# Non-local attention block: theta and phi projected with packed weight halves, and a unit matmul for the correction

## The reference

```python
theta = einsum('bhwc,cd->bhwd', x, W_theta)          # 1024 pixels x 32
phi = maxpool2x2(einsum('bhwc,cd->bhwd', x, W_phi))  # 256 keys x 32
g = maxpool2x2(einsum('bhwc,cd->bhwd', x, W_g))      # 256 keys x 128
beta = softmax(einsum('bqd,bkd->bqk', theta, phi))
tmp = einsum('bqk,bkv->bqv', beta, g)
return gamma * einsum('bhwv,vc->bhwc', tmp, W_o) + x
```

## Time and profile before

| what | value |
|---|---|
| median of 3 runs | 248.03 us (247.55 to 249.0) |
| the profiled execution | 248.0 us, of which the span of the trace is 246.2 us |
| instructions | 4332 |
| busy: PE, DVE, POOL, ACT | 96%, 84%, 69%, 60% of the span |
| clock granted to TensorE | 1.0 |

### The profile page before, as it was taken

How to read it: one execution, slowest core, us unless ns; L and a number is a source line. 1 busy time by engine, 2 the same in 40 slices (tenths; PEclk the granted TensorE clock), 3 DMA queues, 4 the chain that set the end, 5 groups by cost and what they waited for, 6 DMA issues and landing times.

```text
span 246.2 us, 4332 instructions
## 1 busy us (share of the span) xinstructions
PE 235.7 (96%) x1464; PEld 210.4 (85%) x1464; DVE 205.8 (84%) x473; ACT 148.1 (60%) x275; POOL 168.7 (69%) x119
## 2 busy tenths in 40 slices
PE   7896999999999999999999999999999999999884
PEld 4675888898989889898989989898998989899774
DVE  4587896988989898898989899898989989898855
ACT  3763865847475684847567484747749474735260
POOL 1596588676868677686958767695876779544480
PEclk9999999999999999999999999999999999999999
DMA  6790009549194775919377592928668391906924
GB/s 221 285 393 18 3 1 313 204 104 386 49 311 177 234 284 124 384 63 337 123 209 303 142 365 77 347 101 270 243 218 296 95 357 70 329 14 226 372 88 173
DMA packets 15078, 51.14 MB, mean 208 GB/s; under 512 B 1872, under 2 KB 2512, under 8 KB 15056
## 3 DMA queue, kind: packets, MB, share of 16 engines
q1 hardware_dynamic: 14368, 50.14, 58.2%
q10 hardware_dynamic: 688, 0.72, 0.8%
HBM read 33.95 MB, written 16.78 MB: 206 GB/s over the span
## 4 chain that ended last, share of the span: by engine, by line
PE 80%; DVE 7%; DMA 4%; ACT 3%; POOL 3%; issue 1%; ACTq 0%; DVEq 0%
PE proj L195 30%; PE out L299 24%; PE shift L299 8%; PE shift L272 6%; PE score L229 5%; PE score L256 4%; DVE neg_parts L577 3%; DMA x_t<-in_xt 2%; POOL e_lo L506 2%; DMA theta<-neg_lo 2%; PE shift L195 1%; DVE out L552 1%; DVE theta L558 1%; POOL x_lo L501 1%; PE proj L188 1%
## 5 line engine op out<-in xcount | busy, mean ns | idle before, releaser
L506 POOL TENSOR_TENSOR e_lo<-e_sb,e_hi 128x512 fp32r<-128x512 f32 x64 | 82.0, 1295 | 50.8 <-ACT e_sb L434 50.8
L501 POOL TENSOR_TENSOR x_lo<-x_t,x_hi 128x1024 fp32r<-128x1024 f32 x31 | 74.3, 2398 | 13.7 <-ACT x_hi L391 13.7
L299 PE MATMUL out<-G_hi,e_lo 128*128 128x258 f32 x188 | 53.2, 283 | 0.5 <-POOL e_lo L506 0.5
L299 PE MATMUL out<-G_hi,e_hi 128*128 128x258 f32 x188 | 53.4, 284 | 0.0
L299 PE MATMUL out<-G_lo,e_hi 128*128 128x258 f32 x188 | 53.3, 283 | 0.0
L603 DVE SCALAR_TENSOR_TENSOR y_sb<-out,r_sum,x_n 128x256 f32<-128x256 f32 x94 | 45.5, 484 | 6.4
L195 PE MATMUL proj<-x_hi,w_hi 128*128 128x512 f32 x122 | 48.4, 396 | 2.3 <-DVE theta L558 2.3
L195 PE MATMUL proj<-x_hi,w_lo 128*128 128x512 f32 x122 | 48.3, 396 | 0.0
L195 PE MATMUL proj<-x_lo,w_hi 128*128 128x512 f32 x122 | 48.2, 395 | 0.0
L431 ACT ACTIVATE e_hi<-shift 128x512 fp32r<-128x512 f32 x64 | 38.5, 601 | 13.5 <-PE shift L272 13.5
L577 DVE TENSOR_REDUCE neg_parts<-score 128x2 f32<-128x512 f32 x64 | 43.6, 685 | 1.3 <-PE score L229 0.4
(11 more groups left out here) (81 smaller groups left out, 386.3 us busy)
## 6 DMA issues: line engine op xcount, KB each, us to landing
x_n<-in_xn SPq DMA_DIRECT2D x32, 512.0 KB, 7.3
x_t<-in_xt SPq DMA_DIRECT2D x31, 512.0 KB, 5.3
out<-y_sb SPq DMA_DIRECT2D x31, 512.0 KB, 6.6
x_t<-in_xt ACTq DMA_DIRECT2D x2, 256.0 KB, 4.7
w_sb<-in_w_proj SPq DMA_DIRECT2D x1, 256.0 KB, 3.7
theta<-neg_hi ACTq DMA_DIRECT2D x16, 4.0 KB
theta<-neg_lo SPq DMA_DIRECT2D x16, 4.0 KB
out<-y_sb SPq DMA_DIRECT2D x1, 256.0 KB, 2.4
```

Source lines behind the costliest of these rows:

```text
L299: last = nc.tensor.matmul(out_bank(i, t)[:, 0:GW], e[:, i % 2, KC * h + k, cells], G[:, i % 3, k, :], start=(n == 0), stop=(n == 3 * KC - 1))
L501: nc.gpsimd.tensor_tensor(x_lo[:, i % 2, h], x_t[:, i % 2, h], x_hi[:, i % 2, h].bitcast(f32), ALU.subtract).then_inc(x_lo_ready, 1)
L506: nc.gpsimd.tensor_tensor(e_lo[:, i % 2, n, :], e_sb[:, n, :], e_hi[:, i % 2, n, :].bitcast(f32), ALU.subtract).then_inc(e_lo_ready, 1)
```

## The change

The theta/phi weight of the host becomes W_theta, W_phi side by side (64 columns), and the split weights go into one tile `w_all`: 64 high columns, then their 64 remainders, then g's high and low parts. `pair(i, h)` replaces `theta_phi`: for each chunk one matmul of x_hi with all 128 columns gives the high product in PSUM rows 0 to 63 and the correction (x_hi times the weight's remainder) in rows 64 to 127; for each chunk one matmul of x_lo with the 64 high columns adds to rows 0 to 63. ACT copies rows 64 to 127 to SBUF (`copy_corr`), and `add_corr` adds them to rows 0 to 63 by a matmul with a 64x64 unit matrix. A half thus takes five matmuls where it took six. ACT casts 32 rows of theta, not 96, and theta's second high copy (rows 64 to 95) is made by a transfer within SBUF, issued by SP (`twin`), for which `scores(i, 0)` waits.

The order changes too. In the loop PE has `scores(b, h)` ahead of the projection and `add_corr(a, h)` behind `shifted(d, 2 + h)`; ACT has both copies, theta casts and `phi_high` woven with the exponentials of d; DVE has `maxima(b, 0)` first and `maxima(b, 1)` after the second `theta_low`. In the head the first loads all come from SP (x, then weights, then x), DVE splits the weights in parts and makes x_lo of the whole first image, W_o is split later, and `theta_low(1, 1)` stands ahead of `neg_low(0)`. The core of the diff:

```diff
-PROJ = P + DV
+PAIR = 2 * DK
+PROJ = PAIR + DV
+VHI, VLO = 2 * PAIR, 2 * PAIR + DV
+PACKED = VLO + DV
...
+            def twin(i):
+                sp.wait_ge(theta_hi_ready, 2 * i + 2)
+                sp.dma_start(theta[2 * DK:THETA, i % 3, :].bitcast(f32),
+                             theta[0:DK, i % 3, :].bitcast(f32)).then_inc(theta_twin[i % 3], 16)
...
+            for h in range(2):
+                load_t(2, h)
             for h in range(2):
                 load_n(0, h)
+            twin(0)
             for h in range(2):
                 load_t(3, h)
+            twin(1)
             max_into_stack(0)
             for s in range(2, B):
                 a, b, d = s, s - 1, s - 2
+                twin(a)
...
+            def pair(i, h):
+                if i == 0 and h == 0:
+                    pe.wait_ge(w_pair_lo_ready, 1)
+                elif i == 1:
                     pe.wait_ge(theta_lo_ready, h + 1)
                     pe.wait_ge(phi_pooled, h + 1)
                 elif i > 1:
                     pe.wait_ge(g_pooled, 2 * (i - 1) + h + 1)
-                pe.wait_ge(x_lo_ready, 2 * i + h + 1)
-                project(i, h, 0, proj[h], tp_ready)
+                if i > 0 or h > 0:
+                    pe.wait_ge(x_lo_ready, 2 * i + h + 1)
+                for c in range(CC):
+                    if i == 0 and h == 0:
+                        pe.wait_ge(x0_hi_ready, c + 1)
+                    last = nc.tensor.matmul(proj[h][:, :], w_all[:, c, 0:P], x_hi[:, i % 2, h, c, :],
+                                            start=(c == 0), stop=(c == CC - 1), skip_group_check=True)
+                last.then_inc(corr_ready, 1)
+                for c in range(CC):
+                    if i == 0 and h == 0:
+                        pe.wait_ge(x0_lo_ready, c + 1)
+                    nc.tensor.matmul(proj[h][0:PAIR, :], w_all[:, c, 0:PAIR], x_lo[:, i % 2, h, c, :],
+                                     start=False, stop=False, skip_group_check=True)
+
+            def add_corr(i, h):
+                if i == 0 and h == 0:
+                    pe.wait_ge(eye_ready, 1)
+                pe.wait_ge(corr_copied, 2 * i + h + 1)
+                nc.tensor.matmul(proj[h][0:PAIR, :], eye[:, :], corr[:, h, :],
+                                 start=False, stop=True, skip_group_check=True).then_inc(tp_ready, 1)
...
+                    pe.wait_ge(theta_twin[i % 3], twins(i))
...
                 a, b, d = s, s - 1, s - 2
                 if s > 2:
                     for h in range(2):
-                        theta_phi(a, h)
                         scores(b, h)
+                        pair(a, h)
                         shifted(d, 2 + h)
+                        add_corr(a, h)
                     for h in range(2):
                         values(a, h)
                         scores(b, 2 + h)
...
             def theta_high(i, h):
                 act.wait_ge(tp_ready, 2 * i + h + 1)
-                nc.scalar.copy(theta[0:THETA, i % 3, HALF * h:HALF * (h + 1)],
-                               proj[h][0:THETA, :]).then_inc(theta_hi_ready, 1)
+                nc.scalar.copy(theta[0:DK, i % 3, HALF * h:HALF * (h + 1)],
+                               proj[h][0:DK, :]).then_inc(theta_hi_ready, 1)
+
+            def copy_corr(i, h):
+                act.wait_ge(corr_ready, 2 * i + h + 1)
+                nc.scalar.copy(corr[:, h, :], proj[h][PAIR:P, :]).then_inc(corr_copied, 1)
...
+            nc.scalar.copy(eye[:, :], ident[0:PAIR, 0:PAIR]).then_inc(eye_ready, 1)
+            copy_corr(0, 0)
             x_high(0, 1)
-            act.wait_ge(wog_ready, 1)
-            nc.scalar.copy(wo_hi[:, :], w_og[:, :]).then_inc(wo_hi_ready, 1)
+            x_high(1, 0)
             theta_high(0, 0)
-            x_high(1, 0)
+            copy_corr(0, 1)
             x_high(1, 1)
             theta_high(0, 1)
             phi_high(0)
+            copy_corr(1, 0)
+            act.wait_ge(wog_ready, 1)
+            nc.scalar.copy(wo_hi[:, :], w_og[:, :]).then_inc(wo_hi_ready, 1)
             theta_high(1, 0)
+            copy_corr(1, 1)
             g_high(0)
             x_high(2, 0)
             theta_high(1, 1)
             x_high(2, 1)
+            neg_high(0)
             phi_high(1)
-            neg_high(0)
             G_high(0)
             g_high(1)
...
+            copy_corr(2, 0)
             exps(0, 0)
             exps(0, 1)
+            theta_high(2, 0)
+            copy_corr(2, 1)
+            G_high(1)
             theta_high(2, 1)
-            G_high(1)
+            exps(0, 2)
             phi_high(2)
-            exps(0, 2)
             exps(0, 3)
             for s in range(2, B):
                 a, b, d = s, s - 1, s - 2
                 if s > 2:
-                    for h in range(2):
-                        theta_high(a, h)
-                        exps(d, 2 + h)
+                    copy_corr(a, 0)
+                    theta_high(a, 0)
+                    copy_corr(a, 1)
+                    exps(d, 2)
+                    theta_high(a, 1)
                     phi_high(a)
+                    exps(d, 3)
...
             def theta_low(i, h):
-                rows, pixels = slice(DK, 2 * DK), slice(HALF * h, HALF * (h + 1))
+                pixels = slice(HALF * h, HALF * (h + 1))
                 dve.wait_ge(theta_hi_ready, 2 * i + h + 1)
-                v.tensor_tensor(theta[rows, i % 3, pixels], proj[h][rows, :], theta[rows, i % 3, pixels].bitcast(f32),
+                v.tensor_tensor(theta[DK:2 * DK, i % 3, pixels], proj[h][0:DK, :], theta[0:DK, i % 3, pixels].bitcast(f32),
                                 ALU.subtract).then_inc(theta_lo_ready, 1)
...
+            thin, wide = slice(0, PAIR), slice(PAIR, PROJ)
+            dve.wait_ge(w_in, 16)
+            split_hi(thin, thin, w_pair_hi_ready)
+            split_lo(slice(PAIR, 2 * PAIR), thin, thin, w_pair_hi_ready, w_pair_lo_ready)
+            split_hi(slice(VHI, VHI + DV), wide, w_g_hi_ready)
+            first_x_low(0)
+            split_lo(slice(VLO, VLO + DV), wide, slice(VHI, VHI + DV), w_g_hi_ready, w_g_lo_ready)
+            first_x_low(1)
+            dve.wait_ge(x_hi_ready, 1)
+            v.tensor_tensor(x_lo[:, 0, 1], x_t[:, 0, 1], x_hi[:, 0, 1].bitcast(f32),
+                            ALU.subtract).then_inc(x0_lo_ready, 1)
...
             phi_pool(1, 1)
+            theta_low(1, 1)
             neg_low(0)
-            theta_low(1, 1)
             phi_low(1)
...
                 a, b, d = s, s - 1, s - 2
                 if s > 2:
+                    maxima(b, 0)
                     for h in range(2):
                         phi_pool(a, h)
                         theta_low(a, h)
-                        maxima(b, h)
+                    maxima(b, 1)
                     phi_low(a)
                     for h in range(2):
```

More of the change, by code:

```diff
@@ L211, in values @@
                     pe.wait_ge(phi_pooled, 2 * i + h + 1)
-                project(i, h, P, value_bank(i, h), g_ready)
+                elif h == 0:
+                    pe.wait_ge(w_g_lo_ready, 1)
+                for c in range(CC):
+                    for n, (w, x) in enumerate(((VHI, x_hi), (VLO, x_hi), (VHI, x_lo))):
+                        last = nc.tensor.matmul(value_bank(i, h)[:, :], w_all[:, c, w:w + DV], x[:, i % 2, h, c, :],
+                                                start=(c == 0 and n == 0), stop=(c == CC - 1 and n == 2))
+                last.then_inc(g_ready, 1)
             def scores(i, n):
                 if n == 0:
+                    pe.wait_ge(theta_twin[i % 3], twins(i))
                     pe.wait_ge(theta_lo_ready, 2 * i + 2)
@@ L310, in _ @@
                 nc.tensor.matmul(score[0][:, :], e_lo[:, 1, 3, 0:P], e_lo[:, 1, 3, :], start=True, stop=True)
-            first_project()
+            pair(0, 0)
             values(0, 0)
-            theta_phi(0, 1)
+            add_corr(0, 0)
+            pair(0, 1)
             values(0, 1)
-            theta_phi(1, 0)
+            add_corr(0, 1)
+            pair(1, 0)
             scores(0, 0)
             scores(0, 1)
-            theta_phi(1, 1)
+            add_corr(1, 0)
+            pair(1, 1)
             scores(0, 2)
             scores(0, 3)
+            add_corr(1, 1)
             values(1, 0)
@@ L326, in _ @@
             values(1, 1)
-            theta_phi(2, 0)
+            pair(2, 0)
             shifted(0, 0)
@@ L331, in _ @@
             shifted(0, 1)
-            theta_phi(2, 1)
+            add_corr(2, 0)
+            pair(2, 1)
             mix(1)
@@ L335, in _ @@
             shifted(0, 2)
+            add_corr(2, 1)
             values(2, 0)
@@ L609, in _, with split_hi, split_lo, first_x_low @@
             v.memset(G_lo[:, :, :, C:GW].bitcast(f32), 0.0).then_inc(fixed_ready, 1)
-            dve.wait_ge(w_in, 16)
-            v.tensor_copy(w_hi[:, :, :], w_sb[:, :, :]).then_inc(w_hi_ready, 1)
-            dve.wait_ge(w_hi_ready, 1)
```

(10 more changed lines are left out.)

35 lines of the change are left out of this document (20 added, 15 removed).

## The result

The changed kernel takes 266.74 us (median of 4 runs, 266.12 to 269.03) against 248.51 (4 runs, 247.55 to 249.62): ratio 1.074, interval 1.067 to 1.081. It is 18.2 us slower. The prediction had the sign, and was 14 us too low and outside its range. The profiled execution took 269.03 us, with a span of 267.0 and a mean granted clock of 0.97, so it is 2.3 us above the median. In it one 4 KB transfer in the tail takes 4.04 us, against 2.60 us in the earlier trace rows.

A forecast was written before the change was run, and what follows sets the result against it. The prediction took PE to bound the loop; 248.0 us, plus 5.0 for longer loop stages, plus 0.1 for the last stage, minus 0.5 in the head, gave 252.6 us, range 243.0 to 261.0.

The forecast's parts named there:

- the sign: Whole kernel: slower, chance 0.65, against 0.10 for the same time and 0.25 for faster.
- PE bounds the loop: Loop stages: PE sets the pace, busy for 99.60 of 99.60 us over seven stages.
- every matmul fewer is worth its spacing if nothing else becomes late: Theta/phi projections: 0.232 us saved per half, 7.4 us for 16 images, if PE stays the bound.
- The round trip of the copy: Each projection half: PE to ACT's 0.58 us copy to add_corr on PE, a wait of 0.13 each.
- the spacing behind the unit matmul: Loop stage: the next matmul follows add_corr at the usual 0.23, scores(b,1) at 1.76 after add_corr at 1.53.
- +0.13: ACT in the loop: exponentials of (d,2) start 0.13 later per stage if nothing overlaps the copy; outside the main sum.
- The wait of values(a, 1): Loop stage: PE waits 0.30 for DVE's theta remainder, behind ACT's late second theta cast.
- Rival 3: PE projections: changing matmul shape on the array costs 0.16, four times a half; some 260.7 us, chance 0.18.
- the landing of the twin: Head: image 0's theta transfer lands near 16.4, losing 0.9; head in sum -0.5, from -2.2 to +1.5.
- The gain of 1.4 in the head: Head, DVE: theta_low(1,1) ahead of neg_low(0) starts 1.4 us sooner, so values(1,1) wait less for it.
- Costed at nothing: ACT's 32 more casts, the 32-row theta cast, the loop's twin transfers, early scores, DVE's order; the tail also 0.
- Rivals 1 and 2: 1: corrections hidden, PE stays the bound, 240.1 or 244.3, chance 0.25. 2: waits cancel the saving, 247 to 249, chance 0.10.

The follow-up runs named there:

- e7: Kernel before with one of the six matmuls of each theta/phi half left out (x_hi chunk 1 with the weight's remainder): 245.69 us, ratio 0.989.
- e6: e5 without ACT's copy of the correction; the unit matmul adds zeros and waits for nothing: 247.77 us, ratio 0.995.
- e5: Changed kernel with the unit matmul padded to 128 rows and image 0's second theta copy made by ACT casts, not a transfer: 258.60 us, ratio 1.038.
- e3: Changed kernel with image 0's second theta copy made by two ACT casts instead of the transfer: 260.70 us, ratio 1.046.
- e2: Changed kernel with the first unit matmul of an image moved behind scores(b,1) in the loop, still 64 rows: 266.80 us, ratio 1.072.
- e11: Kernel before with 31 added matmuls of 64 rows, one ahead of each theta/phi half but the first, result overwritten: 264.01 us, ratio 1.060.
- e12: Kernel before with 31 added matmuls of 128 rows and 64 weight columns, placed as in e11, result overwritten: 253.14 us, ratio 1.018.
- e8: Kernel before with two head swaps: theta_low(1,1) ahead of neg_low(0) on DVE, neg_high(0) ahead of phi_high(1) on ACT: 247.96 us, ratio 0.998.

## Why the prediction was wrong

The account of the 18 us, from the medians: the saved matmuls give 3.6 (e7 against before); the rest of the new program without the copy costs 2.1 (e6 against e7, and e6 starts its first `turn_max` 2.1 later); the copy 10.8 (e5 against e6); the 64 rows 2.1 once the head is mended (e3 against e5) or 3.4 alone; image 0's transfer 6.0. In sum +17.4, against 18.2 measured; the runs come from different chips, and before is 0.8 slower on that of e7. The intervals of the ratios leave each term uncertain by some 2 us.

- **PE bounds the loop** was right, and "every matmul fewer is worth its spacing if nothing else becomes late" was the right condition. Half the saving was out of reach even with nothing added (e7): theta's remainder gained only 0.23, the slack of 0.11 was used up, and the wait brought a late weight load.
- **The round trip of the copy** was sized well. The copy took 0.58 as taken, the first unit matmul started 1.54 into the stage (predicted 1.53), with a wait of 0.14 (0.13).
- **The step that failed in the loop** is the spacing behind the unit matmul: scores(b, 1) at 1.76 were to follow 0.23 behind it and came at 1.92, the second pair at 2.26 instead of 2.00, the second unit matmul at 3.56 instead of 3.29. The copy(a, 1) moved by that 0.27. Behind it the exponentials were not overlapped either (113.17 to 113.77 is 0.60, where I took 0.48; I had named this as +0.13), so the second theta cast and the remainder moved by 0.37 to 0.39. So the remainder ended at 5.78 (predicted 5.41), values(a, 1) started at 5.84 (5.46), with a late second weight load behind it, and the mix came at 11.52 (11.18), e_low(d, 3) having started at 7.03 (6.66). The wait of values(a, 1) was 0.17 (predicted 0.30) and that of the mix 0.2 (0.32), because PE itself came later. A stage became 0.70 longer, not 0.42: over twelve stages 3.4 us too little.
- **Rival 3 had the mechanism and the place, not the size.** Its test ("0.39 rather than 0.23") is met for the change of rows: 0.37. Its four changes a half at 0.16 were wrong: going from 128 to 64 columns and back costs nothing, changing rows from 128 to 64 and back costs 0.33, once a half. The Trainium skill, TensorEngine Tiling (Array Packing), Key Properties, says that changing the tiling mode drains TensorE. The runs agree for a change of rows (e2, e11); for matmuls of 64 columns among ones of 128 they show no cost (e12; 112.97 to 113.42 above).
- **The step that failed in the head**, and the largest error, is the landing of the twin: -0.5 predicted, +8.2 by the first `turn_max`. I let the twin land when the loads ahead of it had passed (16.4). But it was issued only at 15.14, behind its cast, and the DMA engines' share stayed at 1.00 till 20, with x of image 3 issued at 15.80 right behind it. It landed at 20.4. And I gave the idle PE no price, where the clock fell with it.
- **The gain of 1.4 in the head** from theta_low(1, 1) ahead of neg_low(0) was not there (e8: -0.2%, interval -0.7 to +0.2%, which alone would not exclude it; in the trace 0.3 us are left at the fourth `turn_max`).
- **Costed at nothing** rightly: the twins of the loop (median 3.3 us, a stage of cover), the casts of 32 rows. So was the tail, but for the 1.8 of the one profiled execution, 1.4 of it the one slow transfer.
- **Rivals 1 and 2** (PE stays the bound; the waits cancel the saving) did not come about: the second one's time, 247 to 249, is reached by e6, but only without the copy.

What stays open: why e6 brings its first `turn_max` 1.4 us later than before though its theta needs no transfer. Its scores(0, 0) start at 16.28, behind phi's remainder, 0.8 later than before, and its clock is 0.50 from 18 to 20 us; e3 has the late start and the full clock, and is 1.0 late. Why the clock fell in the one and not in the other isn't shown. No run undid the order of the first loads and casts by itself.

## What to carry to other kernels

Before counting a saved matmul, ask how far the next engine that PE waits for is ahead, and how much sooner it will be done with the matmul gone. Here the slack was 0.11 us and the remainder came 0.23 sooner for 0.46 saved, which with a late weight load halved the gain. A round trip PE, ACT, PE inside a half is paid on every engine that stands behind that ACT instruction: 10.8 us here for 32 casts of 0.58. Don't put a matmul of 64 contraction rows among ones of 96 and more, but pad it to 128 with zeros, and put no transfer on the critical path of a head while the loads keep the DMA engines full.

## What the runs showed of the hardware

- A 64-row, 512-column fp32r matmul among ones of 96 to 128 rows costs 0.33 us more than its stream: 0.09 ahead of it, 0.14 behind, 0.10 one further on; in the trace the weights aren't loaded ahead across the change (112.66 and 113.04 in e2). 128 rows by 64 columns costs none of it.
- A matmul that waited for a semaphore has its weight load start with it, not ahead; where that load was of 128 columns (0.19), the next matmul came 0.10 to 0.11 late (116.08 to 116.64 for two in after; 100.77 to 101.11 in e7).
- A 128 KB transfer within SBUF took 5.3 us from SP's queue and 5.7 from ACT's while the mean share of the DMA engines was 1.00; the median of all sixteen in after is 3.3.
- After 4.8 us without a matmul the granted clock was 0.50, which is 1.2 GHz, from 20 to 28 us, although PE was busy 7.56 of those 8. In e3, after a pause of 1.53 (to 16.24), it stayed at 1.00; in e6, after one of 1.72 (to 16.28), it was 0.50 from 17 to 20.
- ACT starts an exponential 0.49 after the one before, though it lasts 0.60. Behind the copy from PSUM rows 64 to 127 to SBUF rows 0 to 63 (0.58 long) the next starts 0.60 to 0.61 later where it reads PSUM (e_hi, G_hi), and 0.48 to 0.49 later where it reads SBUF (12.29 to 12.78 for x_hi, 23.47 to 23.95 for g_hi in after). The Trainium skill, ScalarE: Activation LUTs, What ACT_TABLE_LOAD costs, states an overlap of about 93 ns for ACTIVATE instructions back to back; the exponentials come near it (0.11), the exponential behind the copy does not.
